# Splitting the 125-row and 111-row transfers of a graph kernel in two, and moving one copy by a chunk

## The reference, cut to what matters

```
# layer 0
h = x @ kernel
scores = leaky_relu([h[src], h[dst]] @ kernel_attention)          # one per edge
scores_exp = exp(clip(scores, -2, 2));  denom = segment_sum(scores_exp, src)
out = segment_sum(h[dst] * scores_exp / (denom[src] + EPS), src)
x = layernorm(x + out)
# layer 1
h = relu([x[src], x[dst]] @ Wm1 + bm1);  h = relu(h @ Wm2 + bm2);  messages = h @ Wm3 + bm3
agg = segment_sum(messages, dst) / clip(count(dst), 1)
upd = relu([x, agg] @ Wn1 + bn1) @ Wn2 + bn2
x = layernorm(x + (x + upd))
```

## Time and profile before

| | |
|---|---|
| median of 3 runs | 2083.1 us (2075.94 to 2091.39) |
| the profiled execution | 2084.37 us, of which the span (first to last instruction) is 2082.7 us |
| PE busy | 1702.8 us, 82% of the span |
| DVE, ACT, POOL busy | 1570.0, 1252.1, 1166.0 us |
| mean granted TensorE clock | 0.921 of full speed |
| index_tables | 0 to 61.6 us |
| attention: windows | 61.6 to about 862 us |
| attention: tables stage | about 862 to 982.9 us |
| messages and update | 982.9 to 2082.7 us |
| largest transfers | 125 of `cnt` from `stage` (305.2 KB each), 250 gathers `head_n`, 13 stores each to `table_a` and `table_b` |

### The profile page before, as it was taken

One profiled execution on the slowest core, in us unless ns is written; L12 is line 12 of the kernel. 1 busy time (PEld: TensorE's weight loads), 2 busy tenths in 40 slices (PEclk: granted clock), 3 DMA queues, 4 the chain that ended last, 5 costly groups with the idle time before them and its releaser, 6 DMA issues.

```text
span 2082.7 us, 54661 instructions
## 1 busy us (share of the span) xinstructions
PE 1702.8 (82%) x15435; PEld 1485.3 (71%) x15436; DVE 1570.0 (75%) x3407; ACT 1252.1 (60%) x2294; POOL 1166.0 (56%) x1204
## 2 busy tenths in 40 slices
PE   5466777767676666662899999999999999999986
PEld 3244666555565555541799999999999999999974
DVE  4577878776565556651788888888888888888886
ACT  3114666667777677332576666676667676767641
POOL 3212345545455545211777777777777777777730
PEclk9799988988878778785899999999999999999999
DMA  2112333434444434123544554455445444544421
GB/s 73 32 33 65 94 105 109 117 107 122 113 122 117 120 116 127 55 76 92 147 138 140 139 140 139 139 139 140 138 138 139 139 138 138 140 139 138 139 62 31
DMA packets 138295, 235.98 MB, mean 113 GB/s; under 512 B 24569, under 2 KB 89165, under 8 KB 138230
## 3 DMA queue, kind: packets, MB, share of 16 engines
q0 software_dynamic: 49632, 142.89, 24.5%
q1 hardware_dynamic: 88598, 92.44, 15.4%
HBM read 185.52 MB, written 10.66 MB: 94 GB/s over the span
## 4 chain that ended last, share of the span: by engine, by line
PE 51%; DVE 1%; issue 1%; ACT 0%; DMA 0%; POOL 0%; ACTq 0%; DVEq 0%; POOLq 0%
PE ps L1188 9%; PE ps L1189 9%; PE ps L1194 9%; PE ps L1172 8%; PE psA L1206 6%; PE ps L1180 4%; PE ps L1167 4%; PE ps L927 1%; PE ps L938 0%; PE ps L935 0%; PE psA L946 0%; DVE x L999 0%; DMA ga<-table_a,idx 0%; ACT u L960 0%; DVE stats L1010 0%
## 5 line engine op out<-in xcount | busy, mean ns | idle before, releaser
L1143 POOL DMA_INDIRECT ga<-table_a,idx x784 | 774.5, 988 | 244.9 <-issue 195.9
L1188 PE MATMUL ps<-wm_hi,h_hi 128*128 128x256 f32 x1568 | 420.8, 302 | 0.2 <-ACT h_hi L1239 0.2
L1243 ACT ACTIVATE h<-ps 128x512 bf16<-128x512 f32 x392 | 234.0, 597 | 282.7 <-PE ps L1194 282.7
L1189 PE MATMUL ps<-wm_lo,h_hi 128*128 128x256 f32 x1568 | 384.2, 279 | 0.0
L571 POOL DMA_INDIRECT head_n<-scr_eye,row_at x250 | 288.6, 1154 | 140.8 <-POOL row_at L567 99.1
L1332 DVE SCALAR_TENSOR_TENSOR rest<-ps,h 128x512 f32<-128x512 f32 x392 | 269.6, 688 | 120.1 <-ACT h L1243 117.5
L1188 PEld LDWEIGHTS ps<-wm_hi,h_hi 128*128 128x128 f32 x1568 | 294.4, 188 | 23.5 <-ACT h_hi L1239 1.2
L1189 PEld LDWEIGHTS ps<-wm_lo,h_hi 128*128 128x128 f32 x1568 | 295.5, 188 | 1.6
L623 PE MATMUL psC<-ring_n,ring_m 128*126 x1180 | 241.5, 338 | 54.5 <-DVE ring_n L803 34.0
L1326 DVE SCALAR_TENSOR_TENSOR h_lo<-ps,h_hi 128x512 fp32r<-128x512 f32 x392 | 264.3, 692 | 3.5 <-ACT h_hi L1239 3.5
L708 ACT ACTIVATE stage<-psC 126x626 f32<-126x626 f32 x125 | 86.1, 689 | 300.5 <-PE psC L632 292.7
(11 more groups left out here) (190 smaller groups left out, 2780.0 us busy)
## 6 DMA issues: line engine op xcount, KB each, us to landing
cnt<-stage SPq DMA_DIRECT2D x125, 305.2 KB
dstb<-scr_dst SPq DMA_DIRECT2D x196, 126.0 KB
ga<-table_a,idx POOLq DMA_INDIRECT x784, 2.9
bw<-table_b SPq DMA_DIRECT2D x196, 63.0 KB
table_b<-cnt SPq DMA_DIRECT2D x12, 375.0 KB
head_n<-scr_eye,row_at POOLq DMA_INDIRECT x250, 4.5
table_a<-pr SPq DMA_DIRECT2D x12, 250.0 KB
x<-in_x SPq DMA_DIRECT2D x1, 1562.5 KB
```

Of the source, the lines that this page charges most:

```text
L1143: pool.indirect_dma_start(ga[:, u, k, :], None, table_a, bass.IndirectOffsetOnAxis(ap=idx[:, u, k:k + 1], axis=0)).then_inc(gathered[u][k] ...
L1188: pe.matmul(ps2[q][:, t % 2, :], hi, w_hi[:, k, :], start=False, stop=True, skip_group_check=True)
L1189: pe.matmul(ps2[q][:, t % 2, :], hi, w_lo[:, k, :], start=False, stop=True, skip_group_check=True)
```

## The change: what it does

Each transfer whose rows were no multiple of 16 is issued as two, the first with a multiple of 16 rows: the edge lists as 96 and 15 rows, x, the identity, the two tables' stores and the output as 112 and 13 rows, and `cnt` from `stage` as 16 rows (80 rows of `stage`) and 9 rows (45 of `stage`). Everything that counted 16 for such a transfer now counts 32. And on ACT the copy of a piece of the factors stands one chunk later, at the head of the chunk's work instead of behind the copy of x.

```
+LOAD_ROWS = ((0, 96), (96, REAL_ROWS))
+ROW_PARTS = ((0, 112), (112, BLK))
+ROWS_A = 16
...
             for tile, lst in ((e_src, src), (e_dst, dst)):
-                sp.dma_start(tile[0:REAL_ROWS, :], lst[0:REAL_ROWS * EL].rearrange("(q n) -> q n", n=EL)).then_inc(edges_in, 16)
+                for a, z in LOAD_ROWS:
+                    sp.dma_start(tile[a:z, :], lst[a * EL:z * EL].rearrange("(q n) -> q n", n=EL)).then_inc(edges_in, 16)
...
-            sp.dma_start(T.x1[:, :, :], x.rearrange("(b n) f -> n b f", b=NBLK)).then_inc(loaded, 16)
+            for a, z in ROW_PARTS:
+                sp.dma_start(T.x1[a:z, :, :], x.rearrange("(b n) f -> n b f", b=NBLK)[a:z, :, :]).then_inc(loaded, 16)
...
-            sp.dma_start(scr_eye.rearrange("(k p) n -> p k n", p=BLK), eye[:, :, :]).then_inc(eye_out, 16)
+            for a, z in ROW_PARTS:
+                sp.dma_start(scr_eye.rearrange("(k p) n -> p k n", p=BLK)[a:z, :, :], eye[a:z, :, :]).then_inc(eye_out, 16)
...
-                    sp.dma_start(cnt[u * WIN:(u + 1) * WIN, (v + 1) % 2, :], stage[0:WM, w % 2, 0:SW]).then_inc(stage_out[w % 2], 16)
+                    sp.dma_start(cnt[u * WIN:u * WIN + ROWS_A, (v + 1) % 2, :], stage[0:ROWS_A * SBLK, w % 2, 0:SW]).then_inc(stage_out[w % 2], 16)
+                    sp.dma_start(cnt[u * WIN + ROWS_A:(u + 1) * WIN, (v + 1) % 2, :], stage[ROWS_A * SBLK:WM, w % 2, 0:SW]).then_inc(stage_out[w % 2], 16)
...
-                sp.dma_start(table_a[rows, :].rearrange("(b p) h -> p b h", p=BLK), a_st[:, g % NB, 0:len(blks), :]).then_inc(a_out[g % NB], 16)
+                for p0, p1 in ROW_PARTS:
+                    sp.dma_start(table_a[rows, :].rearrange("(b p) h -> p b h", p=BLK)[p0:p1, :, :], a_st[p0:p1, g % NB, 0:len(blks), :]).then_inc(a_out[g % NB], 16)
...
-                    act.wait_ge(stage_out[w % 2], t * (BPT * WPB * 8) + 16 * (w // 2) + 16)
+                    act.wait_ge(stage_out[w % 2], t * (BPT * WPB * 16) + 32 * (w // 2) + 32)
...
             for c in range(CH + 3):
+                if 2 <= c <= DCUTS + 1:
+                    a, z = some_nodes(c - 2)
+                    act.wait_ge(edges_summed, c - 1)
+                    act.activation(T.inv.rearrange("p (w m) -> p m w", m=WIN)[:, a:z, :],
+                                   psD[:, 0:(z - a) * NWIN].rearrange("p (m w) -> p m w", w=NWIN), ACT.Copy).then_inc(edges_read, 1)
...
-                if 1 <= c <= DCUTS:
-                    a, z = some_nodes(c - 1)
-                    act.wait_ge(edges_summed, c)
-                    act.activation(T.inv.rearrange("p (w m) -> p m w", m=WIN)[:, a:z, :],
-                                   psD[:, 0:(z - a) * NWIN].rearrange("p (m w) -> p m w", w=NWIN), ACT.Copy).then_inc(edges_read, 1)
...
-                        act.wait_ge(b_out[s], 16 * (g // NB))
+                        act.wait_ge(b_out[s], 32 * (g // NB))
...
-            sp.dma_start(rows[:, a // BLK:z // BLK, :], T.x1[:, a // BLK:z // BLK, :]).then_inc(self.out_done, 16)
+            for p0, p1 in ROW_PARTS:
+                sp.dma_start(rows[p0:p1, a // BLK:z // BLK, :], T.x1[p0:p1, a // BLK:z // BLK, :]).then_inc(self.out_done, 16)
```

More of the change, by code:

```diff
@@ L231, in step @@
                 dve.wait_ge(step_done.sem, step_done.inc(ins))
-            dve.wait_ge(edges_in, 64)
+            dve.wait_ge(edges_in, 96)
             dve.tensor_copy(keys[:, 3, :], e_dst[:, :]).then_inc(keys_ready, 1)
@@ L310, in _ @@
                 last.then_inc(keys_turned, 1)
-            pe.wait_ge(loaded, 48)
+            pe.wait_ge(loaded, 64)
             pe.transpose(psT[0][:, 0:P], w_sb[:, :], T.ident[:, :]).then_inc(k_turned, 1)
@@ L514, in _ @@
             for s in range(2):
-                sp.sem_inc(stage_out[s], 16)
+                sp.sem_inc(stage_out[s], 32)
             def body(t, v):
@@ L534, in _ @@
                 sp.wait_ge(a_ready, g + 1)
-                sp.dma_start(table_a[rows, :].rearrange("(b p) h -> p b h", p=BLK), a_st[:, g % NB, 0:len(blks), :]).then_inc(a_out[g % NB], 16)
+                for p0, p1 in ROW_PARTS:
+                    sp.dma_start(table_a[rows, :].rearrange("(b p) h -> p b h", p=BLK)[p0:p1, :, :], a_st[p0:p1, g % NB, 0:len(blks), :]).then_inc(a_out[g % NB], 16)
                 sp.wait_ge(part_ready[2], g + 1)
-                sp.dma_start(table_b[rows, :].rearrange("(b p) h -> p b h", p=BLK),
-                             b_st[:, g % NB, 0:len(blks), :, :].rearrange("p b c h -> p b (c h)")).then_inc(b_out[g % NB], 16)
+                for p0, p1 in ROW_PARTS:
+                    sp.dma_start(table_b[rows, :].rearrange("(b p) h -> p b h", p=BLK)[p0:p1, :, :],
+                                 b_st[p0:p1, g % NB, 0:len(blks), :, :].rearrange("p b c h -> p b (c h)")).then_inc(b_out[g % NB], 16)
             for s in range(NB):
                 stores = (PAIRS - 1 - s) // NB + 1
-                sp.wait_ge(a_out[s], 16 * stores)
-                sp.wait_ge(b_out[s], 16 * stores)
+                sp.wait_ge(a_out[s], 32 * stores)
+                sp.wait_ge(b_out[s], 32 * stores)
         @block.gpsimd
@@ L857, in tables @@
                 if g >= NB:
-                    dve.wait_ge(a_out[s], 16 * (g // NB))
+                    dve.wait_ge(a_out[s], 32 * (g // NB))
                 dve.tensor_tensor(a_st[:, s, 0:i, :], psC[g % 2][0:BLK, 0, 0:i * H].rearrange("p (b h) -> p b h", h=H),
@@ L913, in sync @@
             sp.wait_ge(self.rows_ready, c + 1)
-            sp.dma_start(rows[:, a // BLK:z // BLK, :], T.x1[:, a // BLK:z // BLK, :]).then_inc(self.out_done, 16)
-        sp.wait_ge(self.out_done, 16 * len(self.cuts))
+            for p0, p1 in ROW_PARTS:
+                sp.dma_start(rows[p0:p1, a // BLK:z // BLK, :], T.x1[p0:p1, a // BLK:z // BLK, :]).then_inc(self.out_done, 16)
+        sp.wait_ge(self.out_done, 32 * len(self.cuts))
     def tensor(self, pe):
```

4 lines of the change are left out of this document (2 added, 2 removed).

## The result

The changed kernel takes 2013.1 us (median of 4 runs, 2010.6 to 2020.0), the kernel before, run beside it on the same chip, 2087.2 us (4 runs): the ratio is 0.966, 95% interval 0.961 to 0.971, 74 us faster. The forecast was 1987 us, with a range of 1942 to 2035. So the sign and the range held and the gain was forecast 22 us too large. That miss is itself a sum: index_tables and windows gave 34 us less than forecast, the tables stage 10 us and messages 2 us more.

What follows compares the result with a forecast made beforehand. Messages is bound by PE, attention windows by waits, often for transfers using 5 of 16 DMA engines. Savings of 14 + 49 + 33 = 96 us from 2084.4 give 1988, about 1987 us for the median; range 1942 to 2035.

Steps and rivals of the forecast that it cites:

- How many engines a transfer uses: All split transfers: 125 rows use 5 of 16 DMA engines; parts of 96, 112 and 16 rows would use all 16.
- index_tables, 14 us: Stage up to the barrier at 61.62: earlier edge lists and a faster identity take 14 us off, bounds 10 and 16.
- Everything to the issue of the identity at 49.24 hangs on DVE's chain and moves with it: In index_tables: DVE starts 9 us earlier, and all work up to SP's issue of the identity comes earlier with it.
- Windows, 49 us: Attention windows: two thirds of 73 us of shorter `cnt` and gather waits, 49 us; least 15, most 95.
- the price of `cnt`: Windows: splitting each `cnt` transfer saves 2.3 us undisturbed, taken as 3; 45 of DVE's 67.5 us of waits go.
- rival 1: Parts are not faster, by the rule or a limit at `cnt`'s 25 destination rows; moved copy alone gives 2074 us; chance 0.04.
- Tables stage, 33 us: Stage before messages: faster split stores and the moved copy of the factors save 33 us, bounds 18 and 45.
- The backlog: Tables stage, last copy to start of messages, 15.7 us: stores that find idle engines save 11 us.
- the end: Tables stage, copy of x at 943.87 to last copy, 23.5 us, ACT mostly waiting for stores: 10 us go.
- the seven chunks: Tables stage, 873.20 to 943.87: the moved copy cuts 70.7 us to 53, taken as 58, so 12 us saved.
- Slower by the second issue: Windows: SP's 125 more issues at 0.74 us could cost 93 us, ending at 2130 us; chance 0.03.
- The marks named: Signs expected in the new trace: earlier barrier, full identity share, shorter `cnt` and gather waits, no store or `psD` waits.

## Why the prediction was right, and where it was wrong

- **How many engines a transfer uses** was right: 16 for parts of 112 rows, by the shares 1.05 and 1.04, where 125 rows had five. It carries the tables stage and the sign. The rule that the prediction set against it, that two transfers to disjoint rows aren't worth it, did not hold for the 125 rows of the stores (23.6 us of the tables stage by themselves).
- **index_tables, 14 us, measured 6.2: the failed step is "Everything to the issue of the identity at 49.24 hangs on DVE's chain and moves with it".** The edges did come 8.2 us earlier (for 9), but POOL's `iota_h` of 5.67 us, done before DVE began in the kernel before, now lay beside its second cast, and the identity went out only 2.5 us earlier. Without the two large iotas the barrier comes at 49.8 us, 11.8 gained, between the bounds of 10 and 16. SP's wait fell by 3.3 us, not 5.
- **Windows, 49 us, measured 23.2: the failed step is the price of `cnt`**, "2.3 us are saved on an undisturbed transfer", taken as 3. Alone it saves 0.17 us (5.47 to 5.30), and the waits for `cnt` lost 4 us instead of 45, the gathers 10 instead of 28. I had the row that spoke against it, 16 GB/s per engine for `cnt` against 21 to 25, and put it into rival 1 at 0.04 together with the rule; for `cnt` that rival was true, for the stores it was not, and the two should have stood apart. What shrank most is what no term had, the idle time at register loads (28 us less ahead of `psO`, 24 ahead of `head_m`); that the 23 us came from there fits the runs and is not shown. The term landed above its lower bound of 15 us by luck. With the rows apart, what I forecast happens: 1.8 us less per transfer, waits for `cnt` down by 25 us more, 78 us off the windows of before.
- **Tables stage, 33 us, measured 42.6.** The backlog (9.8 us for 11) and the end (10.8 for 10) were right; the seven chunks gave 22.7 us where I took 12 (58 us, after a sum of 53; 48.0 measured). In the kernel before they also held 9.2 us of waits for stores, two chunks lasting over 12 us, which I had counted only at the end. Rival 1's price for the move alone, about 10 us "since the backlog of stores takes up the rest", was still too much: it is nothing.
- **Slower by the second issue**: no sign of it; with the 125 pairs alone the kernel is 24 us faster.
- **The marks named**: store and `psD` waits gone, identity's share near 1 and messages 5.9 us after the last copy held or nearly so; the barrier at 47, the waits for `cnt` at 20 us and the halved gather waits did not. That the total came within 22 us owes something to luck: two terms were too large, one too small, and the windows' gain came another way than forecast.

## What to carry to other kernels

Price a transfer by both ends: how many engines its row count gives it, and how widely its destination rows lie; either limit hides the other, so cutting a narrow transfer in two may buy nothing until its rows are spread. Look at who else is slowed while such a transfer runs, since most of what it costs may lie with other engines. When work starts earlier, look at what the other engines do at the new time; and of two waits of one engine in one chunk, ask what is left when one alone is gone.

## What the runs showed of the hardware

- 200 KB from 80 rows into 16 whole rows side by side took 3.7 us, into 16 rows 5 partitions apart 2.7 us. From memory it was 3.7 and 3.0.
- A gather that lands after 3.0 us needed 5.5 us beside a 312.5 KB transfer into 25 neighbouring rows, 3.6 beside the same bytes as a pair into rows 5 apart.
- PE idles up to 2.6 us at a load of registers from SBUF, with no wait shown, in kernels whose transfers into `cnt` are whole, and at most 1.0 with pairs. DVE behind the same loads: 26 to 33 us in all against 2 to 7.
- A cast of 112x896 elements on DVE took 5.70 us beside POOL's iota and 0.61 us without it.
- On two of three chips messages took 35 to 38% longer for the same code. Their traces put waits down to "remote", a name that does not occur in the others; why is open.
